# The QKV weight is transposed and centred on TensorE instead of on VectorE, ScalarE and GpSimd

## The chip, the core and the metric

The kernel runs on one core of a Trainium2 chip. Its time is the device time of one execution in microseconds (us); the times given are medians of the runs named. A profile is one execution recorded by the hardware: each row of it is an instruction, or a group of instructions of one source line (L1385 is line 1385 of the kernel before) on one engine. PE is TensorE, and PEld its weight loads; DVE is VectorE, ACT is ScalarE, POOL is GpSimd, SP issues transfers.

## The reference, cut to what matters

One transformer layer on x of 8 batches x 256 tokens x 256 columns: attention with 16 query heads, 4 key and 4 value heads of 128 columns, then a feed-forward part with 8 routed experts and a shared one. Only the start of the attention is touched:

```python
x = layernorm(x)
qkv = einsum("bsh,oh->bso", x, w_qkv)          # w_qkv: 3072 x 256
q, k, v = split(qkv, [2048, 2560], axis=-1)    # heads of 128 columns
q = (q - mean(q)) * rsqrt(var(q) + eps) * qn_g + qn_b    # over a head's 128 columns
k = (k - mean(k)) * rsqrt(var(k) + eps) * kn_g + kn_b
q = q * cos + rotate_half(q) * sin ; k likewise
```

The mean over a head's columns is linear in the weight. So the kernel takes the mean off the weight once ("centres" it), and the projected heads need no mean taken off.

## The kernel before, in words

**Tiling.** A batch has two tiles of 128 tokens. The weight comes in four groups g, one for each key head: 768 columns = key 128, four queries 512, value 128; and in two halves kk of the 256 input columns. A *unit* u is one group for one token tile: 8 units a batch, 64 in all. Each engine has its own program, an order written out by hand as a loop over steps s (two steps a unit), and waits on semaphores; no planner is at work.

**A unit.** TensorE projects it into pQ in two parts (`qkv`, lines 504 to 520: columns 0 to 511, then 512 to 767), each with six matmuls, because every f32 operand is split into a rounded "hi" part and a "lo" rest (`mm3`, lines 458 to 461). ScalarE squares each head with a running sum (`rope`, L976) and copies the value. VectorE multiplies by two rotary tables TA and TC (L1436, L1441). GpSimd (lines 2003 to 2023) takes the root of the variances (L1999, L2001), adds the two products (L2013), scales by the root (L2016) and adds a third table TB (L2023). Unit 1 alone has those last three on VectorE (`rope_end`, L1409 to L1417). TensorE then transposes the heads (`qk_T`, L527); from step 8 on the scores, the softmax and the output projection of earlier heads are woven in.

**The weight, before.** The weight arrives with the input columns on the partitions, so that it is ready to be multiplied. For each of the 8 pieces (g, kk):

- the means of its five query and key heads: on VectorE for g = 0 (`wq_mean0`, L1369, L1372), on ScalarE for the others (`wq_mean`, L939: five activations with a running sum);
- VectorE subtracts them in place (`wq_centre`, L1380);
- ScalarE rounds to the hi part (`wq_hi`, L945);
- VectorE subtracts the hi part to get the lo part (`wq_lo`, L1385); for the first piece GpSimd does this (L2170).

The steps at which the pieces of g = 2 and 3 are handled stand in the dictionaries MEAN, CENTRE, HI and LO. A unit's projection waits for the lo parts of its group (`s_wqlo_p`, `s_wqlo_d`).

**The rotary tables, before.** TA, TB and TC have five heads each for both token tiles t. GpSimd (t = 0, and TB of t = 1) and VectorE (TA and TC of t = 1, L1392) write the key's head and one query head (`put`), and ScalarE spreads the query head to the three others (`spread`, L955): six spreads.

**PSUM.** Eight banks: pQ two, pT, pS0, pS1, pP, pA, pO one each. The scores' and probabilities' banks are not used until step 8.

Of the kernel before, what the change touches and what calls it, by code (L numbers as in the profile page):

```python
# [14 lines left out]
H = 16  # L15
HKV = 4
# [99 lines left out]
def program(nc, x_d, wqkv_d, wo_d, gb_d, sw_d, ew_d, cs_d, const_d, route_d, spare_d, out_d):  # L116
    with ExitStack() as ctx:
# [31 lines left out]
        tables = part(ropes, 0, 3840).rearrange("p (v t h d) -> p v t h d", v=3, t=2, h=5)  # L149
        t2 = part(ropes, 3840, 2 * QKW).rearrange("p (z c) -> p z c", z=2)  # L150
        t1 = part(ropes, 5120, 3 * QKW).rearrange("p (z c) -> p z c", z=3)
        TA, TB, TC = (tables[:, i, :, :, :] for i in range(3))
        TAB = {"A": TA, "B": TB, "C": TC}
        const = sb("const", [128, 384])
        ident = const[:, 0:128]
        mask = const[:, 128:384]
# [7 lines left out]
        wmean = sb("wmean", [128, 4, 10])  # L164
# [46 lines left out]
        for c, (a, b) in enumerate(CHUNKS):  # L211
# [60 lines left out]
                for (a, b), p in zip(CHUNKS, (pQ[:, 768:1024], pS[1], pS[1]))]  # L272
# [16 lines left out]
        s_dconst, s_dtab = sem("s_dconst"), sem("s_dtab")  # L289
# [18 lines left out]
        s_wmean_a, s_wqhi, s_spread, s_wohi, s_swhi, s_ewhi = (  # L308
            sem(n) for n in ("s_wmean_a", "s_wqhi", "s_spread", "s_wohi", "s_swhi", "s_ewhi"))
# [26 lines left out]
        s_half, s_gain, s_tab_p, s_tabB_p, s_wqlo_p = (  # L336
            sem(n) for n in ("s_half", "s_gain", "s_tab_p", "s_tabB_p", "s_wqlo_p"))
# [118 lines left out]
        def _(e):  # L456
# [42 lines left out]
            def qkv(u, y):  # L499
# [1826 lines left out]
```

## Time and profile before

| | |
|---|---|
| time, three runs | 679.14, 680.0, 681.01 us (median 680.0) |
| span of the profiled execution, first to last instruction | 677.7 us |
| what lies around the span, by those three runs | 1.4 to 3.3 us |
| busy share of the span: PE, PEld, DVE, ACT, POOL | 93%, 86%, 83%, 83%, 82% |
| mean granted TensorE clock, share of full speed | 0.986 |
| instructions | 15538 |

The time of the profiled execution itself is not recorded apart from its span. Shares over the whole span are averages: the start, the attention (up to about 500 us) and the feed-forward part have different limits. The first 15 us are mostly transfers and the first weights.

### The profile page before, as it was taken

How to read it: one execution, taken by the hardware profiler on the slowest of the kernel's cores; microseconds unless marked ns; L12 is line 12 of the kernel's file. 1: busy time of each engine (PE TensorE's matmuls, PEld its weight loads, DVE VectorE, ACT ScalarE, POOL GpSimd, SP SyncE). 2: the span in 40 equal slices, each digit the busy share in tenths (PEclk: the TensorE clock that was granted, in tenths of full speed). 3: DMA queues.
4: the chain of work that ended last, by engine and by line, in shares of the span. 5: the costliest groups of instructions: out<-in, count | busy, mean ns of one | idle time of the engine just before them, and what ended most of it. 6: DMA issues, size and time to landing. Idle time of an engine off the chain costs nothing.

```text
span 677.7 us, 15538 instructions
## 1 busy us (share of the span) xinstructions
PE 631.1 (93%) x4430; PEld 582.2 (86%) x4430; DVE 564.6 (83%) x1925; ACT 565.3 (83%) x2175; POOL 554.9 (82%) x590
## 2 busy tenths in 40 slices
PE   3668999999999999999999999999889999999993
PEld 2557899999999999999999999899779889999981
DVE  6899999998988889888988989988989865555576
ACT  5779999999989999998999999899898536666643
POOL 5799889999999999999999998999877424666654
PEclk9789999999999999999999999999899999999998
DMA  9001023999440000000000000000346123443163
GB/s 346 7 1 33 21 83 108 334 335 291 4 46 1 2 2 2 1 1 1 2 2 1 2 1 1 2 1 25 111 132 220 56 83 116 127 127 120 71 257 124
DMA packets 50978, 54.20 MB, mean 80 GB/s; under 512 B 19824, under 2 KB 42608, under 8 KB 50768
## 3 DMA queue, kind: packets, MB, share of 16 engines
q1 hardware_dynamic: 47488, 43.84, 22.3%
q0 software_dynamic: 3408, 9.38, 3.7%
q8 instruction: 38, 0.62, 0.4%
q14 instruction: 44, 0.36, 0.2%
HBM read 23.76 MB, written 29.51 MB: 79 GB/s over the span
## 4 chain that ended last, share of the span: by engine, by line
POOL 55%; PE 26%; ACT 8%; DVE 5%; issue 4%; DMA 0%; ACTq 0%; DVEq 0%; POOLq 0%
POOL ropes L2023 12%; POOL ropes L2013 12%; POOL ropes L2016 10%; POOL rs L2001 9%; POOL hrow L2037 3%; PE pQ L459 2%; PE pQ L461 2%; PE pQ L460 2%; POOL osb L2044 2%; PE pO L459 2%; ACT ropes L976 2%; POOL rs L1999 2%; PE pO L460 2%; PE pO L461 2%; ACT P L991 2%
## 5 line engine op out<-in xcount | busy, mean ns | idle before, releaser
L459 PE MATMUL pQ<-W 128*128 128x512 f32 (+2 forms) x334 | 119.2, 357 | 10.2 <-DVE W L1385 5.3
L991 ACT ACTIVATE P<-P,nmx 128x128 f32<-128x128 f32 (+1 forms) x256 | 120.3, 502 | 0.0
L460 PE MATMUL pQ<-W 128*128 128x512 f32 (+2 forms) x334 | 114.2, 342 | 0.0
L461 PE MATMUL pQ<-W 128*128 128x512 f32 (+2 forms) x334 | 113.8, 341 | 0.0
L999 ACT ACTIVATE P<-P,rinv 128x128 f32<-128x128 f32 (+1 forms) x256 | 107.2, 492 | 2.5 <-DVE rinv L1468 2.3
L2013 POOL TENSOR_TENSOR ropes<-ropes 128x640 f32<-128x640 f32 x63 | 99.3, 1577 | 6.2 <-DVE ropes L1441 6.2
L2023 POOL TENSOR_TENSOR ropes<-ropes 128x640 f32<-128x640 f32 x63 | 100.3, 1591 | 4.9
L976 ACT ACTIVATE ropes<-pQ 128x128 f32<-128x128 f32 x320 | 89.8, 311 | 13.8 <-POOL ropes L2023 8.0
L459 PE MATMUL pO<-W 128*128 128x256 f32 (+1 forms) x323 | 95.1, 295 | 6.4 <-DVE W L1477 4.7
L1472 DVE TENSOR_TENSOR W<-pP,W 128x384 fp32r<-128x384 f32 x128 | 70.2, 549 | 29.5 <-ACT W L1004 29.2
L460 PE MATMUL pO<-W 128*128 128x256 f32 (+1 forms) x323 | 91.4, 283 | 0.0
L461 PE MATMUL pO<-W 128*128 128x256 f32 (+1 forms) x323 | 91.3, 283 | 0.0
L2016 POOL TENSOR_TENSOR ropes<-ropes,rs 128x640 f32<-128x640 f32 x63 | 81.2, 1290 | 4.9
L2001 POOL TENSOR_TENSOR rs<-rs,half 128x5 f32<-128x5 f32 x64 | 77.4, 1209 | 5.3
L459 PEld LDWEIGHTS pQ<-W 128*128 128x128 f32 x334 | 65.4, 196 | 16.5 <-issue 4.6
L976 ACT ACTIVATION_READ_ACCUMULATOR ropes<-pQ 128x1 f32 x320 | 75.7, 243 | 0.0
L459 PEld LDWEIGHTS pO<-W 128*128 128x128 f32 x323 | 61.4, 190 | 13.8 <-DVE W L1477 7.8
L461 PEld LDWEIGHTS pQ<-W 128*128 128x128 f32 x334 | 65.0, 195 | 6.0
L1004 ACT ACTIVATE W<-pP 128x384 fp32r<-128x384 f32 x128 | 67.5, 527 | 2.0 <-PE pP L551 1.7
L460 PEld LDWEIGHTS pQ<-W 128*128 128x128 f32 x334 | 65.4, 196 | 2.9
L2135 POOL DMA_INDIRECT ys<-ropes x39 | 38.9, 997 | 33.4 <-ACT ropes L1127 25.0
L551 PE MATMUL pP<-const,P 128*128 128x128 f32 x384 | 63.5, 275 | 1.3 <-DVE W L1472 1.2
(268 smaller groups left out, 2209.9 us busy)
## 6 DMA issues: line engine op xcount, KB each, us to landing
xs<-stage SPq DMA_DIRECT2D x1, 17550.0 KB, 58.4
stage<-xs SPq DMA_DIRECT2D x39, 130.0 KB, 2.3
ropes<-in_ew SPq DMA_DIRECT2D x8, 608.0 KB, 4.9
stage<-in_wqkv SPq DMA_DIRECT2D x3, 768.0 KB, 8.2
stage<-ys SPq DMA_DIRECT2D x4, 512.0 KB, 6.3
ropes<-ys SPq DMA_DIRECT2D x4, 512.0 KB, 7.5
out<-X SPq DMA_DIRECT2D x7, 256.0 KB, 2.0
X<-in_wo SPq DMA_DIRECT2D x1, 1536.0 KB, 12.8
```

What stands on the lines that cost most here:

```text
L459: e.matmul(out, lh, rh, start=start, stop=False, skip_group_check=True)
L460: e.matmul(out, lh, rl, start=False, stop=False, skip_group_check=True)
L461: return e.matmul(out, ll, rh, start=False, stop=stop, skip_group_check=True)
L976: a = e.activation(t2[:, z, h * D:h * D + D], pQ[:, h * D:h * D + D], ACT.Square, accum_out=ss[:, z, h:h + 1])
L991: a = e.activation(P[:, z, span(t)], P[:, z, span(t)], ACT.Exp, bias=nmx[:, z, t:t + 1], scale=-1.0, accum_out=sums[:, z, t:t + 1])
L999: a = e.activation(P[:, z, span(t)], P[:, z, span(t)], ACT.Copy, scale=rinv[:, z, t:t + 1])
L1004: e.activation(PT[:, 0, n % 2, :], pP[:, 0:384], ACT.Copy).then_inc(s_PThi, 1)
L1472: e.tensor_tensor(PT[:, 1, n % 2, :], pP[:, 0:384], f(PT[:, 0, n % 2, :]), ALU.subtract).then_inc(s_PT, 1)
L2001: e.tensor_tensor(dst, dst, half[:, 0:n], ALU.pow).then_inc(s_root, 1)
L2013: e.tensor_tensor(t1[:, z3, :], t1[:, z3, :], t2[:, z, :], ALU.add).then_inc(s_add, 1)
L2016: e.tensor_tensor(v3, v3, rs[:, z, :].unsqueeze(2).to_broadcast([128, 5, D]), ALU.mult).then_inc(s_mul, 1)
L2023: e.tensor_tensor(v3, v3, TB[:, t, :, :], ALU.add).then_inc(s_rope, 1)
```

## The change

TensorE now does what three engines did. The host hands the weight over with the output columns of a head on the partitions, and a second constant matrix I - 1/128 ("centring"). Multiplying a raw 128 x 128 block by it on TensorE in true f32 transposes it and takes the mean off in one product; the value's block is only transposed. `centre(i)`, i = 2g + kk, makes one piece: five f32 matmuls and one transpose into two PSUM banks that are idle at the start (those of the scores for kk = 0, those of the probabilities and the output projection for kk = 1). ScalarE's `wq_hi` and VectorE's `wq_lo` read the result from PSUM. All lo parts are VectorE's. Means, in-place centring and their two dictionaries go.

The columns of a group are now four queries, key, value. TA and TC hold one query and one key head and are read by VectorE with a broadcast over the heads; only TB is still spread (two spreads). TB of t = 1 moves from GpSimd to VectorE (`bias_table1`). The mask has its own transfer later in SP's queue, the constants come ahead of the weight, and the gains' scaling is ScalarE's first work.

```diff
-MEAN = {(2, 0): 4, (2, 1): 5, (3, 0): 7, (3, 1): 8}
-CENTRE = {(2, 0): 5, (2, 1): 5, (3, 0): 9, (3, 1): 9}
-HI = {(2, 0): 6, (2, 1): 6, (3, 0): 9, (3, 1): 10}
-LO = {(2, 0): 6, (2, 1): 7, (3, 0): 10, (3, 1): 11}
+CENTRE = {0: [2], 1: [3], 3: [4, 5], 5: [6], 6: [7]}
+HI = {1: [2], 2: [3], 4: [4], 5: [5], 6: [6], 7: [7]}
+LO = {2: [2], 3: [3], 4: [4], 5: [5], 6: [6], 7: [7]}
...
+        pSS = pb("pSS", 1024)
+        pPO = pb("pPO", 1024)
+        pW = [pSS[:, 0:GW], pPO[:, 0:GW]]
...
         @block.sync
             e.dma_start(X[:, 0:2, :], x_d[:, 0:2, :]).then_inc(s_dx[0], 16)
-            for kk in range(2):
-                e.dma_start(raw_q[0][:, kk, :], wqkv_d[:, 0, kk, :]).then_inc(s_dwq[kk], 16)
-            e.dma_start(const[:, :], const_d).then_inc(s_dconst, 16)
-            e.dma_start(cs[:, :, :, :], cs_d).then_inc(s_dtab, 16)
-            e.dma_start(gb[:, :, :], gb_d).then_inc(s_dtab, 16)
+            e.dma_start(const[:, 0:256], const_d[:, 0:256]).then_inc(s_dconst, 16)
+            e.dma_start(raw_q[0][:, 0, :], wqkv_d[:, 0, 0, :]).then_inc(s_dwq[0], 16)
+            e.dma_start(gb[:, :, :], gb_d).then_inc(s_dgb, 16)
+            e.dma_start(raw_q[0][:, 1, :], wqkv_d[:, 0, 1, :]).then_inc(s_dwq[1], 16)
+            e.dma_start(cs[:, :, :, :], cs_d).then_inc(s_dcs, 16)
             for g in range(1, HKV):
                 e.dma_start(raw_q[g], wqkv_d[:, g, :, :]).then_inc(s_dwq[g + 1], 16)
+            e.dma_start(mask, const_d[:, 256:512]).then_inc(s_dmask, 16)
...
         @block.tensor
+            def centre(i):
+                g, kk = divmod(i, 2)
+                e.wait_ge(s_dwq[kk if g == 0 else g + 1], 16)
+                if i == 0:
+                    e.wait_ge(s_dconst, 16)
+                if i >= 2:
+                    e.wait_ge(s_wqlo, i - 1)
+                for h in range(5):
+                    e.matmul(pW[kk][:, h * D:h * D + D], raw_q[g][:, kk, h * D:h * D + D], centring, start=True,
+                             stop=True, skip_group_check=True)
+                e.transpose(pW[kk][:, QKW:GW], raw_q[g][:, kk, QKW:GW], ident).then_inc(s_wcen, 1)
...
+            centre(0)
             ln1_T(0)
+            centre(1)
             for s in range(WOVEN):
                 if s < QFIRST:
                     qkv(s // 2, s % 2)
                 if 0 <= tu < NU:
                     qk_T(tu, tr)
+                for i in CENTRE.get(s, []):
+                    centre(i)
...
         @block.scalar
-            wq_hi(0, 0)
+            e.wait_ge(s_dgb, 16)
+            e.activation(gb[:, 0:2, :], gb[:, 0:2, :], ACT.Copy, scale=float(D) ** -0.5).then_inc(s_gain, 1)
+            wq_hi(0)
             ln1_hi(0)
-            e.wait_ge(s_dtab, 32)
-            e.activation(gb[:, 2:4, :], gb[:, 2:4, :], ACT.Copy, scale=float(D) ** -0.5).then_inc(s_gain, 1)
-            wq_hi(0, 1)
-            wq_mean(1, 0)
-            spread(0, "A")
-            spread(0, "C")
+            wq_hi(1)
...
+                for i in HI.get(s, []):
+                    wq_hi(i)
+                if s in (2, 3):
+                    spread(s - 2)
...
         @block.vector
+            def wq_lo(i):
+                g, kk = divmod(i, 2)
+                e.wait_ge(s_wqhi, i + 1)
+                e.tensor_tensor(WQ[:, g, 1, kk, :], pW[kk], f(WQ[:, g, 0, kk, :]), ALU.subtract).then_inc(s_wqlo, 1)
...
-                e.tensor_tensor(t1[:, z3, h0 * D:h1 * D], pQ[:, h0 * D:h1 * D],
-                                TA[:, t, h0:h1, :].rearrange("p h d -> p (h d)"), ALU.mult)
+                e.tensor_tensor(t1[:, z3, h0 * D:h1 * D].rearrange("p (h d) -> p h d", d=D),
+                                pQ[:, h0 * D:h1 * D].rearrange("p (h d) -> p h d", d=D),
+                                TA[:, t, y:y + 1, :].to_broadcast([128, n, D]), ALU.mult)
...
             ln1_stats(0)
-            wq_mean0(0)
-            wq_centre(0, 0)
             ln1_apply(0)
-            wq_mean0(1)
-            wq_centre(0, 1)
+            wq_lo(0)
             ln1_lo(0)
-            wq_lo(0, 1)
-            table1("A")
-            table1("C")
+            wq_lo(1)
+            scale_tables1()
...
                 if s == 2:
-                    wq_centre(1, 0)
-                    wq_centre(1, 1)
+                    bias_table1()
                 if s == 4:
-                    wq_lo(1, 0)
-                    wq_lo(1, 1)
                     rope_end(1)
+                for i in LO.get(s, []):
+                    wq_lo(i)
```

On GpSimd the lo part of the first piece (L2170) and TB of t = 1 go; the tables of t = 0 stay.

## Rows read from the trace of the kernel before

**Rows 1.** Whole core by stretch: busy us of each engine and (x instructions), then PE clock.
```profile
15.20:40.80 25.60, 16.71 (x71) 13.25 (x71) 22.79 (x44) 19.76 (x108) 21.02 (x21) 0.87 0.08 34
40.80:58.50 17.70, 11.94 (x66) 9.17 (x65) 17.16 (x47) 14.29 (x57) 17.22 (x14) 0.90 0.03 6
58.50:79.80 21.30, 19.97 (x138) 17.67 (x138) 21.20 (x65) 21.08 (x83) 19.09 (x16) 1.00 0.06 23
79.80:139.50 59.70, 58.91 (x435) 55.46 (x433) 54.88 (x200) 56.08 (x239) 54.70 (x52) 1.00 0.56 177
```

**Rows 2.** Timeline of POOL at the start: start us, duration us, instruction (units 0, 2, 3, 5).
```profile
20.03 1.54 POOL L2013 TENSOR_TENSOR ropes<-ropes 128x640 f32<-128x640 f32 x1
...
32.57 1.56 POOL L2013 TENSOR_TENSOR ropes<-ropes 128x640 f32<-128x640 f32 x1
...
40.87 1.55 POOL L2013 TENSOR_TENSOR ropes<-ropes 128x640 f32<-128x640 f32 x1
...
52.93 3.69 POOL L2037 TENSOR_SCALAR hrow<-X,mv,lr 128x256 f32<-128x256 f32 x2
...
58.47 1.58 POOL L2013 TENSOR_TENSOR ropes<-ropes 128x640 f32<-128x640 f32 x1
```

**Rows 3.** Waits from 15.2 to 39.2 us: in total, times, longest.
```profile
PE pQ L459 <- DVE W L1385: 4.4, 2, 3.5
...
POOL rs L1999 <- ACT ropes L976: 3.6, 1, 3.6
...
DVE ropes L1436 <- ACT ropes L976: 3.2, 3, 1.7
```

**Rows 4.** Groups by line, DVE, 15.2 to 39.2 us: busy us, mean ns, idle before.
```profile
L1385 DVE TENSOR_TENSOR W<-stage,W 128x768 fp32r<-128x768 f32 x4 | 5.4, 1364 | 0.0
...
L1380 DVE TENSOR_TENSOR stage<-stage,wmean 128x640 f32<-128x640 f32 x4 | 3.5, 912 | 0.0
```

**Rows 5.** Groups by line, DVE, 40.8 to 58.5 us.
```profile
L1385 DVE TENSOR_TENSOR W<-stage,W 128x768 fp32r<-128x768 f32 x2 | 3.2, 1593 | 0.0
L1380 DVE TENSOR_TENSOR stage<-stage,wmean 128x640 f32<-128x640 f32 x2 | 3.0, 1522 | 0.0
```

**Rows 6.** Timeline of the first 20 us, four instructions, with [idle before].
```profile
4.94 0.82 DVE L1369 TENSOR_REDUCE wmean<-stage 128x5 f32<-128x640 f32 x1
...
9.66 3.88 POOL L2029 TENSOR_TENSOR ropes<-P,osb 128x256 f32<-128x256 f32 x4
...
15.27 0.69 DVE L1436 TENSOR_TENSOR ropes<-pQ,ropes 128x512 f32<-128x512 f32 x1 [1.12 <-ACT ropes L976]
...
17.68 0.66 POOL L1999 TENSOR_SCALAR rs<-ss 128x5 f32<-128x5 f32 x1
```

**Rows 7.** Timeline of PE: matmuls at the two clocks, and one f32 product.
```profile
14.07 0.41 PE L460 MATMUL pQ<-W 128*128 128x256 f32 x1
...
14.29 0.41 PE L461 MATMUL pQ<-W 128*128 128x256 f32 x1
...
27.28 0.28 PE L460 MATMUL pQ<-W 128*128 128x256 f32 x1
...
27.40 0.28 PE L461 MATMUL pQ<-W 128*128 128x256 f32 x1
...
659.17 1.02 PE L754 MATMUL pS<-ropes,const 128*128 128x512 f32 x2
```

**Rows 8.** Timeline of POOL later on, two units in a row and one layer norm.
```profile
112.37 2.44 POOL L2037 TENSOR_SCALAR hrow<-X,mv,lr 128x256 f32<-128x256 f32 x2
...
139.46 1.57 POOL L2013 TENSOR_TENSOR ropes<-ropes 128x640 f32<-128x640 f32 x1
...
145.43 1.58 POOL L2013 TENSOR_TENSOR ropes<-ropes 128x640 f32<-128x640 f32 x1
```

**Rows 9.** Groups by line up to 54 us: ACT's means, DVE's tables.
```profile
L939 ACT ACTIVATE W<-stage 128x128 fp32r<-128x128 f32 x30 | 8.9, 315 | 0.0
...
L1392 DVE TENSOR_TENSOR ropes<-P,osb 128x128 f32<-128x128 f32 (+1 forms) x3 | 1.9, 681 | 0.0
```

More of the change, by code:

```diff
@@ L148, in program @@
         ropes = sb("ropes", [128, 7040])
-        tables = part(ropes, 0, 3840).rearrange("p (v t h d) -> p v t h d", v=3, t=2, h=5)
+        TB = part(ropes, 0, 1280).rearrange("p (t h d) -> p t h d", t=2, h=5)
+        TA = part(ropes, 1280, 512).rearrange("p (t h d) -> p t h d", t=2, h=2)
+        TC = part(ropes, 1792, 512).rearrange("p (t h d) -> p t h d", t=2, h=2)
         t2 = part(ropes, 3840, 2 * QKW).rearrange("p (z c) -> p z c", z=2)
         t1 = part(ropes, 5120, 3 * QKW).rearrange("p (z c) -> p z c", z=3)
-        TA, TB, TC = (tables[:, i, :, :, :] for i in range(3))
-        TAB = {"A": TA, "B": TB, "C": TC}
-        const = sb("const", [128, 384])
+        const = sb("const", [128, 512])
         ident = const[:, 0:128]
-        mask = const[:, 128:384]
+        centring = const[:, 128:256]
+        mask = const[:, 256:512]
         hrow = sb("hrow", [128, 2, HID])
@@ L176, in program @@
         pT = pb("pT", 512)
-        pS = [pb("pS0", 512), pb("pS1", 512)]
-        pP = pb("pP", 512)
+        pSS = pb("pSS", 1024)
+        pS = [pSS[:, 512 * z:512 * z + 512] for z in range(2)]
+        pPO = pb("pPO", 1024)
+        pP, pO = pPO[:, 0:512], pPO[:, 512:1024]
         pA = pb("pA", 512)
-        pO = pb("pO", 512)
+        pW = [pSS[:, 0:GW], pPO[:, 0:GW]]
         raw_q = [stage[:, 1536 * g:1536 * g + 1536].rearrange("p (k c) -> p k c", k=2) for g in range(HKV)]
@@ L1394, in put, with scale_tables1, bias_table1 @@
                 return a
-            def table1(which):
-                dst = TAB[which][:, 1, :, :]
-                if which == "A":
-                    e.wait_ge(s_gain, 1)
-                    put(dst, cs[:, 0, 1, :], 0, False).then_inc(s_tab_d, 1)
-                else:
-                    put(dst, cs[:, 1, 1, :], 0, True).then_inc(s_tab_d, 1)
+            def scale_tables1():
+                e.wait_ge(s_gain, 1)
+                e.wait_ge(s_dcs, 16)
+                put(TA[:, 1, :, :], cs[:, 0, 1, :], 0, False).then_inc(s_tab_d, 1)
+                put(TC[:, 1, :, :], cs[:, 1, 1, :], 0, True).then_inc(s_tab_d, 1)
+            def bias_table1():
+                put(TB[:, 1, 3:5, :], cs[:, 0, 1, :], 1, False)
+                put(ctmp[:, 1, :, :], cs[:, 1, 1, :], 1, True).then_inc(s_tab_d, 1)
+                e.wait_ge(s_tab_d, 3)
+                e.tensor_tensor(TB[:, 1, 3:5, :], TB[:, 1, 3:5, :], ctmp[:, 1, :, :], ALU.add).then_inc(s_tab_d, 1)
             def rope_end(u):
@@ L2265 @@
     i = np.arange(128)
+    centring = ident - f32(1.0 / D)
     mask = np.where(i[None, :] > i[:, None], f32(-2e38), f32(0)).astype(f32)
@@ L2315 @@
         "x": x, "wqkv": wqkv, "wo": wo, "gb": gb, "sw": sw, "ew": ew, "cs": cs,
-        "const": np.concatenate([ident, 0 * mask, mask], axis=1), "route": route,
+        "const": np.concatenate([ident, centring, 0 * mask, mask], axis=1), "route": route,
         "spare": spare,
```

141 lines of the change are left out of this document (46 added, 95 removed).

## The prediction

> **What bounds the kernel now.** I first read the busy time by stretch [rows 1]. From 79.8 us TensorE is busy 58.91 of 59.70 us: the attention proper is TensorE's, and its instructions are the same after the change. What the change touches lies earlier. From 58.5 to 79.8 VectorE has no gap (21.20 of 21.30 us), and before 58.5 no engine is the limit alone: TensorE is idle 25.60 - 16.71 = 8.9 us of the stretch from 15.2 to 40.8, and 5.8 us of the next.
>
> The waits of that first stretch [rows 3] tell why: TensorE waits 4.4 us for lo parts of the weight (L1385), GpSimd 3.6 us and VectorE 3.2 us for ScalarE's squares, which stand behind ScalarE's 30 mean activations of 0.315 us each [rows 9]. So the making of the weight sits on VectorE and ScalarE in front of the first units, while TensorE idles.
>
> How far a delay there reaches, I read from GpSimd's timeline, the chain of waits running along it: unit 0's add starts at 20.03, unit 2's at 32.57, unit 3's at 40.87, unit 5's at 58.47 [rows 2]. Later a unit alone takes GpSimd 145.43 - 139.46 = 5.97 us [rows 8]. The two units from 40.87 to 58.47 take 17.60 with one layer norm between them. GpSimd was busy for all but 0.5 us of it [rows 1], but with stretched instructions: that layer norm took 3.69 us there [rows 2] and 2.44 later [rows 8]. They stretch while VectorE subtracts with both inputs in SBUF, and VectorE's do too: the centrings of that stretch took 1.522 us each, against 0.912 in the earlier one, and the lo parts 1.593 and 1.364 [rows 4, 5].
>
> **The change, part by part.**
>
> *A f32 product on TensorE.* The trace has one kind: 512 columns by the identity, two records in 1.02 us [rows 7]. For 128 columns I take two records at the spacing of 256-column matmuls, because each record of an f32 product streams at half pace: 0.12 us at the high clock, 0.22 at the low one [rows 7]; the second spacing is that of the 1.2 GHz level, though the column of the granted clock says 1.00 there. A product then costs 0.24 us, and a piece (five products, one transpose) 1.3; at the low level 0.44 and 2.3 to 2.4. Eight pieces are some 10.5 us at the high clock.
>
> The footnote to the table of engine peaks in the Trainium skill (Perfetto Trace Analysis, Engine Utilization) gives TensorE half its output rate for an f32 product in low and high halves. The row shows two such records for each product, a quarter of the rate. By the page a piece would cost about 0.7 us, and unit 0 would come up to 1.2 us earlier than I put it; I go by the row.
>
> *Unit 0.* The first weights are in by 4.94 us at the latest, when VectorE sums them [rows 6]; the constants now go ahead of them, so I start `centre(0)` at 5.6. TensorE was idle then, so 2.3 us at the low clock cost nothing but order: the transpose of the input waits until 7.9, `centre(1)` runs from 8.9 to 11.2. ScalarE's hi (0.85) and VectorE's lo follow each. The lo part reads one operand from PSUM; the nearest row is the 512-column product of that sort, 0.69 us [rows 6], so for 768 columns at most 1.04: I take 1.0. The second lo part is then ready at about 13.1, and the first half of unit 0's projection ends between 13.9 (high clock) and 14.9 (low), so VectorE's first rotary product starts between 15.1 and 16.2, against 15.27 [rows 6]. Nothing is won up to here. `centre(2)` is queued ahead of the projection's second half and delays its squares to 16.7 (high) or 19.2 (low). GpSimd's work on unit 0 began at 17.68, after tables that began at 9.66 [rows 6]. It loses a lo part and three of the six table pieces, and ends its tables at about 14. Unit 0's add starts at 18.1 or 20.7, against 20.03.
>
> *VectorE up to unit 3.* From 15.27 to unit 3's products (39.3 us) it loses four centrings, 3.5 us; its four lo parts of 5.4 us become six of 1.0, and TB of t = 1 comes to it: four operations of about 0.68 [rows 4, 9], 2.7 us. Net 3.5 + 5.4 - 6.0 - 2.7 = 0.2 us less. What is to win is the 3.2 us of waiting for squares [rows 3]. All of it, if TensorE and ScalarE are always ahead; nothing, if VectorE now waits for TensorE's centrings instead. TensorE's six remaining pieces (2 to 7) take 7.8 us of its 8.9 idle ones at the high clock, so they fit; ScalarE loses 30 x 0.315 us and more [rows 9], so squares stand behind hi parts alone. I take half, 1.6. With 0.2 that is 1.8, and I round to 2.0 for the faster start of GpSimd. Bounds: 3.6 won (all waits gone, high clock) and 0.7 lost (no wait gone, first product 0.9 late).
>
> *Units 3 to 5.* VectorE loses 3.2 + 3.0 = 6.2 us here [rows 5]: the last two centrings are gone, and the last two lo parts are already made. With it goes what they did to GpSimd, which then paces this stretch: two units of 5.97 and a layer norm of 2.44 are 14.4 us, 3.2 less than 17.60. If the subtractions for the output weight, which stay, still stretch the layer norm to 3.69, it is 2.0 less. I take 2.6. VectorE's 17.16 - 6.2 and TensorE's 11.94 us of work [rows 1] fit in 15.
>
> *What costs nothing.* The rotary products read TA and TC by broadcast, in all units. The centring read a broadcast too, and its 640 columns took 0.912 us with contention, no more than the products' 0.69 for 512 would make; I put it at zero, covered by VectorE's 4.8 us of idle time in 79.8 to 139.5 [rows 1]. Without that cover, 0.02 us on each of 128 products would be 2.6 us. Four spreads on ScalarE go, off the path. The mask's own transfer lands long before step 8. `row_ends` and the route's transfer on SP now wait for the pieces, which are ready earlier.
>
> *The sum.* 2.0 + 2.6 = 4.6 us. From 58.5 on VectorE and then TensorE work without gaps on the same instructions, so the lead is neither eaten nor enlarged. The profiled span of 677.7 becomes 673.1; the median of the three runs lies 2.3 above that span, and so I forecast 675.4. The bounds, -0.7 + 2.0 = 1.3 and 3.6 + 3.2 = 6.8 us, are 678.7 and 673.2.
>
> A measurement of this kernel can tell about 0.3%, 2.0 us, from no change.
>
> **The rivals.**
>
> *The lead is given back* (679 to 681). If, past 58.5, the pace is not the work but a wait that stays where it is, all is hidden. For it: VectorE's 21.20 of 21.30 us looks like a floor, and the subtractions for the output weight fall into that stretch, in a new overlap with GpSimd. Against it: that work is not tied to a clock time; it begins when the steps before it end. Its transfer was issued at the start and is long there.
>
> *TensorE becomes the bound of the start* (slower). If the clock stays at the low level while it centres, the six pieces take 13.8 to 14.4 us, and 8.9 of idle time don't hold them: some 4.9 us or more stand in front of unit 3 instead of the 2.0 won. With half of the 2.6 behind it still won, that is 3.6 us slower, 683.6. It decides from a piece of 8.9 / 6 = 1.5 us on, little above my 1.3. For it: TensorE ran long parts of this start at the low level [rows 7], and the mean clock of 0.87 shows it [rows 1]. Against it: the centrings fill the very gaps after which the clock had fallen, and at the high clock TensorE's own matmuls of this stretch shrink too.
>
> *More than forecast* (under 673). If GpSimd isn't the pace from unit 3 to 5, VectorE's whole 6.2 us count, up to 3.6 + 6.2 = 9.8 us, 670.2. ScalarE's 14.29 us in that stretch [rows 1], only some 1.7 of them hi parts that move away, speak against most of it.
>
> *The broadcast costs.* If VectorE reads a repeated operand slower, every unit pays, but TensorE is the pace there: it would need more than the 4.8 us of slack to show. I put it with the slower cases, at 682.6 if its 2.6 us came on top.
>
> **How the numbers follow.** The forecast's case, 1.3 to 6.8 us won: 0.70, of which 0.06 goes to the part under 2.0 us. More than 6.8: 0.07. Given back, within 2 us of 680.0: 0.13. TensorE the bound: 0.06; the broadcast and what I don't see: 0.04. So faster 0.64 + 0.07 = 0.71, same 0.06 + 0.13 = 0.19, slower 0.10. The range, 672.5 to 680.0, leaves out the larger gain, the slower cases and the upper edge of the hidden case; the forecast's own is 673.2 to 678.7.
>
> **What the profile after would show.** Right: pieces of 1.3 us on TensorE in its former gaps; the wait of TensorE for L1385 shorter than 4.4 us; unit 3's add on GpSimd near 38.9 us and unit 5's near 53.9; from there the same distances as before, with VectorE's products no longer than 0.69 us. Wrong in the first term, if unit 3's add is not earlier than 40.87; in the second, if units 3 to 5 still take 17 us; in the carrying, if unit 5's add is 4 us earlier and the end is not. The forecast fails as a whole if a piece takes 2 us on TensorE throughout, or if another engine, ScalarE first, has no gap from 40 us on.

## The result, and the profile after

The changed kernel takes 674.81 us (median of four runs, 673.5 to 675.87; before 679.9 in the same session). The ratio is 0.9925, interval 0.9909 to 0.9941: 4.0 to 6.2 us faster. The forecast was 675.4. The profiled execution took 675.87 us with a span of 673.8, 3.9 less than the 677.7 before.

The busy time by stretch answers to [rows 1]; the columns are the same.

```profile
15.20:40.80 25.60, 20.43 (x141) 17.65 (x139) 22.17 (x49) 15.13 (x67) 18.63 (x18) 1.00 0.12 51
40.80:58.50 17.70, 14.32 (x82) 12.00 (x80) 15.63 (x52) 15.81 (x64) 17.06 (x15) 0.90 0.09 31
58.50:79.80 21.30, 20.39 (x145) 18.28 (x145) 21.30 (x67) 20.67 (x84) 18.26 (x14) 1.00 0.06 14
79.80:139.50 59.70, 59.17 (x432) 55.62 (x432) 54.88 (x204) 56.02 (x235) 54.72 (x53) 1.00 0.63 199
```

From 15.2 to 40.8 TensorE is busy 20.43 us instead of 16.71, at a granted clock of 1.00 instead of 0.87, and ScalarE 15.13 instead of 19.76. VectorE is hardly freer (22.17 for 22.79) in that stretch; it does more of the attention in it.

GpSimd's timeline answers to [rows 2]: unit 0, the next products of units 2 and 3, the layer norm, units 5, 8 and 63.

```profile
18.25 1.81 POOL L1990 TENSOR_TENSOR ropes<-ropes 128x640 f32<-128x640 f32 x1
...
30.79 1.56 POOL L1990 TENSOR_TENSOR ropes<-ropes 128x640 f32<-128x640 f32 x1 [1.44 <-DVE ropes L1427]
32.44 1.26 POOL L1993 TENSOR_TENSOR ropes<-ropes,rs 128x640 f32<-128x640 f32 x1
...
35.40 0.19 POOL L1976 TENSOR_SCALAR lr<-mv 128x2 f32<-128x2 f32 x1
...
37.89 1.57 POOL L1990 TENSOR_TENSOR ropes<-ropes 128x640 f32<-128x640 f32 x1
...
48.36 2.89 POOL L2014 TENSOR_SCALAR hrow<-X,mv,lr 128x256 f32<-128x256 f32 x2
...
53.03 1.57 POOL L1990 TENSOR_TENSOR ropes<-ropes 128x640 f32<-128x640 f32 x1
...
60.05 1.57 POOL L1990 TENSOR_TENSOR ropes<-ropes 128x640 f32<-128x640 f32 x1 [0.61 <-DVE ropes L1427]
...
75.23 1.57 POOL L1990 TENSOR_TENSOR ropes<-ropes 128x640 f32<-128x640 f32 x1 [0.89 <-DVE ropes L1427]
...
475.54 1.58 POOL L1990 TENSOR_TENSOR ropes<-ropes 128x640 f32<-128x640 f32 x1
```

The same view of the kernel before, for what [rows 2] don't show:

```profile
34.21 1.85 POOL L2016 TENSOR_TENSOR ropes<-ropes,rs 128x640 f32<-128x640 f32 x1
...
37.79 0.78 POOL L1999 TENSOR_SCALAR lr<-mv 128x2 f32<-128x2 f32 x1
...
79.82 1.57 POOL L2013 TENSOR_TENSOR ropes<-ropes 128x640 f32<-128x640 f32 x1 [0.90 <-DVE ropes L1441]
...
480.14 1.58 POOL L2013 TENSOR_TENSOR ropes<-ropes 128x640 f32<-128x640 f32 x1
```

The reading that carries the rest is to take differences between units. Unit 0's add comes 1.78 us earlier. From there to unit 2 both kernels take 12.54, which is a coincidence, as VectorE's timeline below shows. From unit 2 to unit 3 it is 7.10 instead of 8.30, and the 1.20 are two instructions: the product with the root takes 1.26 instead of 1.85, the first step of a root 0.19 instead of 0.78. From unit 3 to 5 it is 15.14 instead of 17.60. That makes a lead of 5.44 at unit 5. Between units 5 and 8 GpSimd waits for VectorE's product, and 0.85 is given back; from unit 8 (4.59) to unit 63 (4.60) nothing changes. In the traces of the twelve kernels below the lead grows by 0.37 to 0.55 between these two, so half a microsecond is within what single traces leave open.

The waits from 15.2 to 39.2 us answer to [rows 3].

```profile
ACT ropes L986 <- PE pQ L461: 7.7, 4, 3.2
POOL rs L1976 <- ACT ropes L986: 5.7, 2, 3.0
...
PE pPO L472 <- DVE W L1364: 1.7, 2, 1.2
...
PE pSS L472 <- DVE W L1364: 1.4, 2, 1.3
...
DVE ropes L1421 <- ACT ropes L986: 1.4, 2, 1.0
```

TensorE's 4.4 us for lo parts have become 3.1, now in front of the pieces (L472) instead of the projections. VectorE waits 1.4 for squares instead of 3.2, but GpSimd 5.7 instead of 3.6: unit 2's squares are late because ScalarE waits 7.7 us for TensorE in this stretch. Why, TensorE's timeline tells (pieces 0, 2 and 5, and unit 2's projection):

```profile
6.28 2.50 PE L472 MATMUL pSS<-const,stage 128*128 128x128 f32 x10 [6.28 <-DMA stage<-in_wqkv]
...
14.05 1.28 PE L472 MATMUL pSS<-const,stage 128*128 128x128 f32 x10
15.17 0.27 PE L474 MATMUL pSS<-const,stage 128*128 128x128 f32 x1
15.19 0.36 PE L459 MATMUL pQ<-W 128*128 128x256 f32 x1
...
22.28 1.35 PE L472 MATMUL pPO<-const,stage 128*128 128x128 f32 x10 [1.17 <-DVE W L1364]
...
23.49 0.47 PE L459 MATMUL pQ<-W 128*128 128x512 f32 x1
```

Each f32 product is two records. A piece at the high clock holds TensorE 15.19 - 14.05 = 1.14 us, while piece 0, at the 1.2 GHz level, takes twice that (the level is read from the spacing of its records; the clock column says 1.00 there). Unit 2's projection stands behind piece 5, and piece 5 behind a lo part.

These late squares don't set unit 2, though. With its root done, GpSimd waits another 1.44 us for VectorE's product (30.79 above). VectorE's timeline in the changed kernel (its first product, and its last for unit 2), its busy time between, and its last product for unit 2 in the kernel before:

```profile
15.43 0.69 DVE L1421 TENSOR_TENSOR ropes<-pQ,ropes 128x512 f32<-128x512 f32 x1 [0.95 <-ACT ropes L986]
...
30.43 0.28 DVE L1427 TENSOR_TENSOR ropes<-pQ,ropes 128x128 f32<-128x128 f32 x1
```

```profile
19.98:30.79 10.81, 7.74 (x57) 6.62 (x56) 10.66 (x18) 5.36 (x20) 6.11 (x7) 1.00 0.01 2
```

```profile
32.01 0.28 DVE L1441 TENSOR_TENSOR ropes<-pQ,ropes 128x128 f32<-128x128 f32 x1
```

VectorE is busy for 10.66 of the 10.81 us up to unit 2's add: it sets unit 2 now. From its first product (15.43, before 15.27) to this last one it takes 15.00 us instead of 16.74. So unit 2's 1.78 us come from VectorE's shorter waits, not from the earlier unit 0, behind which GpSimd waits again.

### The profile page after: what moved, and what is told of

It is laid out like the page before. It is cut to its first block, busy times and chain, and to the rows that moved or that the text cites. A ratio compares the mean times of both kernels' runs of the same rounds, so it can differ in the third digit from the quotient of the medians.

```text
span 673.8 us, 15649 instructions
## 1 busy us (share of the span) xinstructions
PE 636.3 (94%) x4518; PEld 589.2 (87%) x4518; DVE 553.9 (82%) x1918; ACT 555.4 (82%) x2111; POOL 543.9 (81%) x585
## 4 chain that ended last, share of the span: by engine, by line
POOL 50%; PE 28%; ACT 9%; DVE 6%; issue 5%; DMA 1%; SPq 0%; ACTq 0%; DVEq 0%; POOLq 0%
POOL ropes L1990 11%; POOL ropes L2000 11%; POOL ropes L1993 9%; POOL rs L1978 9%; PE pQ L459 3%; POOL hrow L2014 3%; PE pQ L461 3%; PE pQ L460 3%; ACT ropes L986 2%; POOL osb L2021 2%; PE pPO L459 2%; ACT P L1001 2%; PE pPO L460 2%; PE pPO L461 2%; POOL rs L1976 1%
## 5 line engine op out<-in xcount | busy, mean ns | idle before, releaser
L459 PE MATMUL pQ<-W 128*128 128x512 f32 (+2 forms) x334 | 116.4, 349 | 2.1 <-DVE W L1364 0.8
L460 PE MATMUL pQ<-W 128*128 128x512 f32 (+2 forms) x334 | 111.8, 335 | 0.0
L461 PE MATMUL pQ<-W 128*128 128x512 f32 (+2 forms) x334 | 111.4, 333 | 0.0
L459 PE MATMUL pPO<-W 128*128 128x256 f32 (+1 forms) x323 | 95.7, 296 | 5.6 <-DVE W L1465 3.6
L1460 DVE TENSOR_TENSOR W<-pPO,W 128x384 fp32r<-128x384 f32 x128 | 70.2, 549 | 30.2 <-ACT W L1014 30.0
L460 PE MATMUL pPO<-W 128*128 128x256 f32 (+1 forms) x323 | 91.9, 285 | 0.0
L461 PE MATMUL pPO<-W 128*128 128x256 f32 (+1 forms) x323 | 91.7, 284 | 0.0
L459 PEld LDWEIGHTS pPO<-W 128*128 128x128 f32 x323 | 61.9, 192 | 12.8 <-DVE W L1465 6.7
L459 PEld LDWEIGHTS pQ<-W 128*128 128x128 f32 x334 | 63.6, 190 | 6.6 <-DVE W L1364 1.2
L1014 ACT ACTIVATE W<-pPO 128x384 fp32r<-128x384 f32 x128 | 67.1, 524 | 2.4 <-PE pPO L565 2.2
L461 PEld LDWEIGHTS pQ<-W 128*128 128x128 f32 x334 | 63.3, 190 | 5.6
L460 PEld LDWEIGHTS pQ<-W 128*128 128x128 f32 x334 | 63.7, 191 | 2.6
L1437 DVE TENSOR_TENSOR W<-pT,W 128x384 fp32r<-128x384 f32 (+1 forms) x128 | 61.5, 480 | 5.2 <-ACT W L994 5.1
```

Source lines behind the costliest of these rows:

```text
L459: e.matmul(out, lh, rh, start=start, stop=False, skip_group_check=True)
L460: e.matmul(out, lh, rl, start=False, stop=False, skip_group_check=True)
L461: return e.matmul(out, ll, rh, start=False, stop=stop, skip_group_check=True)
L1014: e.activation(PT[:, 0, n % 2, :], pP[:, 0:384], ACT.Copy).then_inc(s_PThi, 1)
L1460: e.tensor_tensor(PT[:, 1, n % 2, :], pP[:, 0:384], f(PT[:, 0, n % 2, :]), ALU.subtract).then_inc(s_PT, 1)
```

## The experiments

Every kernel below was timed against the kernel before, in sessions of one to four kernels; the kernel before took 679.86 to 680.61 us in them (medians). The changed kernel was timed only in its own session, so it is compared with the others by the ratios; where two intervals overlap, the times don't tell the two kernels apart. The table gives the differences in GpSimd's timeline (us), the lead over the kernel before at units 8 and 63, and the times. In the changed kernel and its variants the first weights land between 5.9 and 6.9 us, so a single trace places unit 0 to about half a microsecond; the differences between units don't hang on that.

| kernel | unit 0 | 0 to 2 | 2 to 3 | 3 to 5 | 5 to 8 | lead at 8 | at 63 | time | ratio, interval |
|---|---|---|---|---|---|---|---|---|---|
| before | 20.03 | 12.54 | 8.30 | 17.60 | 21.35 | | | 679.9 | |
| after | 18.25 | 12.54 | 7.10 | 15.14 | 22.20 | 4.59 | 4.60 | 674.81 | 0.9925, 0.9909 to 0.9941 |
| tables_alone | 17.96 | 17.48 | 8.27 | 17.60 | 21.35 | -2.84 | -2.32 | 682.01 | 1.0025, 1.0012 to 1.0039 |
| weight_alone | 18.02 | 12.60 | 7.09 | 15.12 | 21.34 | 5.65 | 6.03 | 674.46 | 0.9922, 0.9907 to 0.9936 |
| warm_before | 20.89 | 13.26 | 8.29 | 17.58 | 21.36 | -1.56 | -1.07 | 681.85 | 1.0031, 1.0017 to 1.0044 |
| double_centre | 23.06 | 14.27 | 7.81 | 15.11 | 21.36 | -1.79 | -1.24 | 679.3 | 0.9995, 0.9985 to 1.0005 |
| act_mean | 19.04 | 12.91 | 7.67 | 15.11 | 22.20 | 2.89 | 3.41 | 675.24 | 0.9926, 0.9911 to 0.994 |
| dve_sub | 18.85 | 12.54 | 7.08 | 17.64 | 21.36 | 2.35 | 2.72 | 675.86 | 0.9937, 0.9921 to 0.9953 |
| dve_red | 18.32 | 12.55 | 7.08 | 14.84 | 22.22 | 4.81 | 5.21 | 674.43 | 0.991, 0.9896 to 0.9924 |
| transp | 16.27 | 12.66 | 7.11 | 15.12 | 21.46 | 7.20 | 7.73 | 673.35 | 0.9906, 0.9885 to 0.9927 |
| tb_pool | 17.70 | 12.62 | 7.08 | 15.13 | 22.21 | 5.08 | 5.47 | 674.07 | 0.9912, 0.9896 to 0.9929 |
| warm_start | 17.30 | 12.55 | 7.08 | 15.12 | 21.37 | 6.40 | 6.84 | 672.56 | 0.9895, 0.9877 to 0.9913 |
| all_four | 17.06 | 12.15 | 7.08 | 15.14 | 21.35 | 7.04 | 7.52 | 673.32 | 0.9918, 0.9898 to 0.9939 |
| order4 | 18.63 | 13.55 | 7.11 | 15.13 | 22.21 | 3.19 | 3.61 | 675.61 | 0.9941, 0.9927 to 0.9954 |

**The two halves apart.** *tables_alone* is the kernel before with only the new order of columns, the narrow tables, the broadcast reads and TB of t = 1 on VectorE:

```diff
-            spread(0, "A")
-            spread(0, "C")
...
-                e.tensor_tensor(t1[:, z3, h0 * D:h1 * D], pQ[:, h0 * D:h1 * D],
-                                TA[:, t, h0:h1, :].rearrange("p h d -> p (h d)"), ALU.mult)
+                e.tensor_tensor(t1[:, z3, h0 * D:h1 * D].rearrange("p (h d) -> p h d", d=D),
+                                pQ[:, h0 * D:h1 * D].rearrange("p (h d) -> p h d", d=D),
+                                TA[:, t, y:y + 1, :].to_broadcast([128, n, D]), ALU.mult)
...
+                    bias_table1()
```

*weight_alone* is the changed kernel with the old five-head tables and six spreads, and TB of t = 1 on GpSimd:

```diff
-                if s == 2:
-                    bias_table1()
...
+                if s == 2:
+                    spread(1, "A")
+                    spread(1, "C")
```

> The kernel before with only the table half of the change: query columns first, TA and TC with two heads read by broadcast, two spreads instead of six, TB of t = 1 on VectorE; the weight is prepared as before. Theory W (the lead comes from the weight's preparation leaving VectorE and ScalarE): ScalarE loses four spreads of about 0.55 us, VectorE gets about 1.4 us more, so the time stays within 1 us of the kernel before, about 679.5. Rival T (the lead comes from the smaller tables, which free GpSimd and the squares early): 3 to 5 us faster, 675 to 677.

> The changed kernel with the five-head tables, the six spreads and GpSimd's table work of before put back; the weight is still transposed and centred on TensorE. Theory W: 4 to 5 us faster than before, 675 to 676; unit 3's add on GpSimd still near 38 to 39 us. Rival T: no more than 1 us faster than before, 679 to 680.

The weight half alone gives all of the gain; the table half alone makes the kernel slower, by 2 us where theory W had less than 1. The waits of tables_alone from 15.2 to 39.2 us say where:

```profile
POOL rs L2000 <- ACT ropes L974: 9.7, 3, 7.7
...
PE pQ L459 <- DVE W L1379: 6.0, 1, 6.0
```

VectorE makes TB while the lo parts for unit 2 wait behind it, and the work around it stretches (the two centrings ahead of it take 2.91 us instead of 1.94, the two lo parts 3.07 instead of 1.82). So TensorE's wait for these lo parts grows from 4.4 to 6.0 us and units 0 to 2 take 17.48 us. Either half alone brings unit 0 two microseconds forward, since each takes work from GpSimd's queue ahead of it (a lo part, or TB).

**Is it the clock?** *warm_before* is the kernel before with as many f32 products of the identity, unused, put into TensorE's gaps at the places of the pieces.

```diff
+            def idle_work(i):
+                out = [pS[0], pP][i % 2]
+                for h in range(5):
+                    e.matmul(out[:, 128 * (h % 4):128 * (h % 4) + 128], ident, ident, start=True, stop=True,
...
+                for i in {0: [2], 1: [3], 3: [4, 5], 5: [6], 6: [7]}.get(s, []):
+                    idle_work(i)
```

> The kernel before, with TensorE doing 8 x 5 f32 products of the identity into the idle banks at the places where the changed kernel centres; nobody reads them, and VectorE, ScalarE and GpSimd work as before. Rival C (the lead comes from TensorE's clock, which rises some 8 us earlier because TensorE has work in its gaps): 2 to 4 us faster than before, 676 to 678. Theory W: the matmuls of units 0 to 3 get shorter but wait for the same lo parts, so within 1 us of before, 679 to 681.

```profile
15.20:40.80 25.60, 19.75 (x114) 16.78 (x114) 23.45 (x39) 18.51 (x100) 21.14 (x20) 0.87 0.08 32
```

Slower by 2 us, with units 2 to 3 and 3 to 5 as before: work in TensorE's gaps alone gains nothing. It doesn't settle the clock, for the granted clock of this stretch stayed at 0.87, as before the change, and was 1.00 in the changed kernel. What the higher clock is worth by itself, no run isolates.

**What a piece costs.** *double_centre* issues each of the five products twice (the second overwrites the first).

```diff
-                for h in range(5):
+                for h in [0, 1, 2, 3, 4] * 2:
                     e.matmul(pW[kk][:, h * D:h * D + D], raw_q[g][:, kk, h * D:h * D + D], centring, start=True,
```

> The changed kernel with every f32 product of the centring done twice, so that a piece takes some 2.5 us instead of 1.3 at the high clock. TensorE is idle 5.2 us of 15.2 to 40.8 in the changed kernel, and six pieces bring 7.2 more there. Theory (the piece's price decides from about 1.5 us on, as the prediction has it): 2 to 4 us slower than the changed kernel, 677 to 679. Rival (the pieces hide in TensorE's waits whatever they take): under 1 us slower, up to 675.8.

*transp* has five plain transposes instead of the products, so the centring is left out and the heads keep their means.

```diff
-                    e.matmul(pW[kk][:, h * D:h * D + D], raw_q[g][:, kk, h * D:h * D + D], centring, start=True,
+                    e.transpose(pW[kk][:, h * D:h * D + D], raw_q[g][:, kk, h * D:h * D + D], ident)
```

> The changed kernel with five plain transposes in place of the five f32 products of a piece: the centring is left out, so the heads' means are not taken off. A piece should take about 0.7 us at the high clock and 1.3 at the low one instead of 1.3 and 2.5. Theory H (TensorE's centring is hidden in its gaps but for the first two pieces): unit 0's add about 1 to 1.5 us earlier than 18.25, unit 3's add 0.5 to 1.5 us earlier than 37.9, the kernel 673.3 to 674.5. Rival B (the six later pieces still hold TensorE and with it units 1 to 3): unit 3's add 3 us or more earlier, the kernel under 672.5. Rival N (nothing of the centring is on the path): within 0.5 us of 674.8.

Timeline of TensorE in transp, pieces 0 and 2:

```profile
5.94 1.33 PE L472 MATMUL pSS<-const,stage 128*128 128x128 f32 x5 [5.94 <-DMA stage<-in_wqkv]
...
12.28 0.71 PE L472 MATMUL pSS<-const,stage 128*128 128x128 f32 x5
```

A piece takes half, and what is won is in unit 0 (16.27); up to unit 5 the distances stay as they were. So at the high clock the five later pieces cost nothing, and the first three, which stand in front of unit 0's two projections, do (the medians don't tell this kernel from the changed one). Doubled pieces cost 4.81 us in unit 0 and 2.44 between units 0 and 3 in the trace, which took longest of its twelve executions, and 4.5 us in the medians, more than expected. TensorE is then busy 23.78 of the 25.60 us:

```profile
15.20:40.80 25.60, 23.78 (x181) 21.78 (x180) 18.14 (x37) 11.48 (x48) 12.01 (x12) 1.00 0.12 48
```

**Whose work was the brake?** Three kernels put one thing each back into the changed kernel, unused: ScalarE's thirty means (*act_mean*), four subtractions on VectorE with both operands in SBUF at the steps of the last centrings and lo parts (*dve_sub*), and sums over the same columns there, with one operand (*dve_red*).

The edit of act_mean, and that of dve_sub:

```diff
+            wq_mean(1, 0)
...
+                for g, kk in {2: [(1, 1)], 4: [(2, 0)], 5: [(2, 1)], 7: [(3, 0)], 8: [(3, 1)]}.get(s, []):
+                    wq_mean(g, kk)
```

```diff
+                for kk, n in {9: [(0, 640), (1, 640)], 10: [(0, 768)], 11: [(1, 768)]}.get(s, []):
+                    e.tensor_tensor(raw_q[3][:, kk, 0:n], raw_q[3][:, kk, 0:n], raw_q[2][:, kk, 0:n], ALU.subtract)
```

In dve_red the last line is a sum instead:

```diff
+                    e.tensor_reduce(wsum[:, 2 * (n > 640) + kk, 0:n // D], raw_q[3][:, kk, 0:n].rearrange("p (h d) -> p h d", d=D), AXX,
+                                    ALU.add)
```

> The changed kernel, with ScalarE's thirty mean activations (about 0.32 us each, 9.4 us in all) put back at the steps they had before; nobody reads their results. Theory S (the first term was ScalarE's time: squares stood behind the means): the squares come late again, unit 3's add on GpSimd goes from 37.9 back to 40.5 to 41 us, VectorE waits about 3 us for squares between 15.2 and 39.2, and the kernel takes 677.3 to 678.3 us, the first term of the lead lost and the second kept. Rival V (the first term was VectorE's own centrings and lo parts): unit 3's add within 0.5 us of 37.9, time within 0.7 us of 674.8.

> The changed kernel, with four subtractions of two SBUF operands (two of 640, two of 768 columns) put back on VectorE at the steps where the last two centrings and lo parts stood; results unused. Theory G (between units 3 and 5 these four set the pace, by their time and by stretching GpSimd): unit 3's add stays at 37.9, units 3 to 5 take 17 to 17.6 us again instead of 15.1, the layer norm on GpSimd takes 3.7 us again or more, and the kernel takes 677 to 677.8 us, the second term lost. Rival O (units 3 to 5 got faster by something else, the moved hi parts on ScalarE or the clock): units 3 to 5 within 0.5 us of 15.1, time within 0.7 us of 674.8.

> As the kernel with the four subtractions put back, but each is a sum over the same columns with one SBUF input and a small output, so about the same time on VectorE (0.7 to 0.8 us each, 3.1 us in all) without a second operand. Theory C (the stretch of GpSimd by two-operand work is what cost): units 3 to 5 take at most 15.6 us and the kernel 674.8 to 675.8. Theory P (VectorE's own time paces units 3 to 5 whatever it does): units 3 to 5 take about 18 us less what is idle, some 16.5 to 18, and the kernel 676.5 to 678.

First the two on VectorE. GpSimd's timeline (unit 3, layer norm, unit 5) and VectorE's groups from 36 to 60 us in dve_sub:

```profile
38.47 1.57 POOL L1994 TENSOR_TENSOR ropes<-ropes 128x640 f32<-128x640 f32 x1
...
50.57 3.68 POOL L2018 TENSOR_SCALAR hrow<-X,mv,lr 128x256 f32<-128x256 f32 x2
...
56.11 1.58 POOL L1994 TENSOR_TENSOR ropes<-ropes 128x640 f32<-128x640 f32 x1
```

```profile
L1829 DVE TENSOR_TENSOR stage<-stage 128x768 f32<-128x768 f32 x2 | 2.9, 1458 | 0.0
...
L1829 DVE TENSOR_TENSOR stage<-stage 128x640 f32<-128x640 f32 x2 | 1.9, 1013 | 0.0
```

and the same in dve_red:

```profile
37.95 1.57 POOL L1996 TENSOR_TENSOR ropes<-ropes 128x640 f32<-128x640 f32 x1
...
48.92 2.46 POOL L2020 TENSOR_SCALAR hrow<-X,mv,lr 128x256 f32<-128x256 f32 x2
...
52.79 1.57 POOL L1996 TENSOR_TENSOR ropes<-ropes 128x640 f32<-128x640 f32 x1
```

```profile
L1830 DVE TENSOR_REDUCE wsum<-stage 128x6 f32<-128x768 f32 x2 | 1.9, 952 | 0.0
...
L1830 DVE TENSOR_REDUCE wsum<-stage 128x5 f32<-128x640 f32 x2 | 1.5, 815 | 0.0
```

Four subtractions of 4.8 us bring units 3 to 5 back to 17.64, the layer norm back to 3.68. Sums of 3.4 us over the same columns at the same steps leave 14.84 and 2.46. So in the traces the brake is the second SBUF operand, by what it does to GpSimd, and not VectorE's time. By the Trainium skill (SBUF — State Buffer, Who interferes with whom) a VectorE instruction with two SBUF inputs contends with a GpSimd instruction that reads SBUF, because its second input comes through a read interface that the two share, and one with at most one SBUF input, outside the two-port modes, does not. The two rows of the layer norm agree: 3.68 against 2.46 us. The subtractions also write wide results and the sums don't, but the changed kernel's lo parts write 768 columns from one SBUF operand, and GpSimd's root beside one of them (from 21.64 us) takes 1.18 us, against 1.63 and 1.76 beside two-operand work in the kernel before. In the medians dve_sub lies 1.4 us above dve_red (the executions hardly overlap) and 1.1 above the changed kernel: less than the 2.5 of the traces, and short of theory G's 677 to 677.8. The profiled execution of dve_sub took longest of its six, so how much of the second term the other executions gained stays open.

act_mean's waits from 15.2 to 39.2 us:

```profile
POOL rs L1991 <- ACT ropes L998: 10.5, 3, 5.4
...
DVE ropes L1436 <- ACT ropes L998: 2.4, 2, 1.5
```

Unit 3's add is 1.73 us later (39.62), of which 0.79 stand at unit 0, where piece 1 ran longer at the low level (2.26 us instead of 1.60): less than the 2.6 to 3.1 of the theory, more than its rival's 0.5. Its median (675.24) can't be told from the changed kernel's, although its trace is 1.2 us behind at unit 63; there too the profiled execution took longest. What the means cost the untraced executions stays open.

**Can more be had?** *tb_pool* makes TB of t = 1 on GpSimd again, with the narrow tables. *warm_start* puts fourteen products of a blank block on TensorE while the first transfers run. *order4* moves piece 5 behind unit 2's first projection. *all_four* has all three, and ScalarE rounds piece 0 before it scales the gains.

The three edits in this order:

```diff
-                if s == 2:
-                    bias_table1()
...
-            put(TB[:, 0, 3:5, :], cs[:, 0, 0, :], 1, False)
+            for t in range(2):
+                put(TB[:, t, 3:5, :], cs[:, 0, t, :], 1, False)
```

```diff
+            e.wait_ge(s_blank, 1)
+            for i in range(14):
+                e.matmul(pT[:, 0:128], blank, blank, start=True, stop=True, skip_group_check=True)
             centre(0)
```

```diff
-CENTRE = {0: [2], 1: [3], 3: [4, 5], 5: [6], 6: [7]}
+CENTRE = {0: [2], 1: [3], 3: [4], 4: [5], 5: [6], 6: [7]}
```

> The changed kernel with its narrow tables and broadcast reads, but the third table TB of the second token tile is made on GpSimd again, as before the change. Theory B (the table half's cost is VectorE's four operations for TB in front of unit 1): unit 8's add on GpSimd comes 0.8 to 1.3 us earlier than 75.23, as with the old tables (74.17), and the kernel takes 673.5 to 674.5 us. Rival R (the cost is in the broadcast reads or the fewer spreads, not in where TB is made): unit 8's add within 0.3 us of 75.23 and the time within 0.5 us of 674.8.

> The changed kernel, with fourteen f32 products of a blank 128 x 128 block put on TensorE ahead of the first piece, while the first transfers are under way; nothing reads them. Theory K (the first two pieces took 2.5 and 1.6 us because TensorE came from idleness at the lower clock level, and unit 0 waits for them): the ten records of the first piece take about 1.3 us instead of 2.50, unit 0's add comes 0.8 to 1.3 us earlier than 18.25, and the kernel takes 673.5 to 674.3 us. Rival L (the lower level is not a matter of what ran before, or unit 0 waits for the transfers): the first piece again 2.5 us, or unit 0's add within 0.3 us of 18.25; time within 0.5 us of 674.8.

> The two edits above together (TB of the second tile on GpSimd, fourteen blank products ahead of the first piece), and two more: piece 5 is put on TensorE one step later, behind unit 2's projection, and ScalarE rounds piece 0 before it scales the gains. If the gains add up, unit 0's add is at about 17.0, unit 8's at 72.5 to 73.3 instead of 75.23, and the kernel takes 672.0 to 673.3 us. Rival: VectorE, without a gap from 58.5 on in the changed kernel, already sets units 5 to 8, and what comes earlier in front of it is waited away: unit 8's add at 74 or later, time 673.8 or more.

> The changed kernel with one piece moved: piece 5 is put on TensorE one step later, behind unit 2's first projection instead of ahead of it. In the trace of the changed kernel unit 2's projection starts at 23.49 us, 1.4 us after its last lo part was done (22.13), because piece 5 stands in front of it. Theory Q (TensorE's queue holds unit 2 there): from unit 0's add to unit 2's the time falls from 12.54 us to 11.1 to 12.1, unit 2's projection starts at 22.2 to 22.5, and the lead reaches unit 8; time 673.4 to 674.4 us. Rival V (VectorE sets unit 2: its last steps for unit 1, the 640-column product of 2.08 us among them, stand in front of unit 2's products): 12.3 to 12.6 us, time within 0.5 us of 674.8.

warm_start is the fastest, 679.91 - 672.56 = 7.35 us below the kernel before in its session; its interval of the ratio just touches the changed kernel's. TensorE's first two pieces in it:

```profile
6.87 1.38 PE L474 MATMUL pSS<-const,stage 128*128 128x128 f32 x10 [0.57 <-DMA stage<-in_wqkv]
...
8.90 1.38 PE L474 MATMUL pPO<-const,stage 128*128 128x128 f32 x10
```

Piece 0 takes 1.38 instead of 2.50 us, and although its weights landed 0.59 us later than in the trace of the changed kernel, unit 0's add comes 0.95 earlier. The 0.85 given back between units 5 and 8 is gone too. tb_pool gains 0.49 at unit 8, less than expected, all of it in unit 0, where a single trace can't tell; its median can't be told from the changed kernel's. all_four leads by another 0.64 at unit 8 but is not faster than warm_start in the medians.

order4 failed in an instructive way. Unit 2's projection starts at 21.69 instead of 23.49, as Q wanted, yet units 0 to 2 take 13.55 us. TensorE's timeline (piece 6) and the stretch:

```profile
27.79 2.40 PE L472 MATMUL pSS<-const,stage 128*128 128x128 f32 x10 [1.96 <-DVE W L1364]
```

```profile
15.20:40.80 25.60, 21.51 (x138) 18.86 (x136) 21.25 (x47) 14.58 (x65) 17.30 (x17) 0.93 0.11 45
```

VectorE took no notice of the earlier projection: its first product for unit 2 starts 7.21 us after its first for unit 1 (27.56 and 20.35), in the changed kernel 7.23 (27.21 and 19.98). So far rival V was right, that VectorE sets unit 2. The extra microsecond comes behind that: TensorE idled 1.96 us for VectorE's lo part, piece 6 then ran at the 1.2 GHz level, 2.40 us instead of 1.35, and VectorE waited 1.12 us for a copy of ScalarE's whose transposes stood behind piece 6. Neither theory had that. The wait alone doesn't decide it: in all_four, which has the same order after a warm start, TensorE waits the same 1.96 us, piece 6 takes 1.35, the clock stayed at 1.00 in this stretch and the distance is 12.15. order4's median, 675.61, can't be told from the changed kernel's.

## Why the prediction was right, step by step

**The piece.** Forecast 1.3 us at the high clock and 2.3 to 2.4 at the low one; measured 1.14 (15.19 - 14.05) and 2.51 (from 6.28 to the next matmul at 8.79). The row's quarter rate held. By the half rate in the Trainium skill's footnote (Perfetto Trace Analysis, Engine Utilization) a product would, as an estimate, take what a transpose takes. The trace disagrees: in transp five transposes are five records in 0.71 us, in the changed kernel five products ten records in 1.28.

**Unit 0.** The add was put at 18.1 or 20.7; it came at 18.25. VectorE's first rotary product came at 15.43 (forecast 15.1 to 16.2), the lo part from PSUM took 0.95 us (forecast 1.0). TB's four operations took VectorE 1.31 us in all (forecast 2.7).

**The first term: right in its place, mis-sized by a cause that I had left out.** I put 2.0 us up to unit 3's add; it is 2.98. Up to unit 2 the mechanism is the forecast's, and so is the size: 1.78 us, VectorE's waits for squares shrinking by 1.8 (3.2 to 1.4) while its work hardly changes. The 1.8 us of unit 0 were rightly not counted on top: GpSimd waits again behind them, 3.02 us for squares and 1.44 for VectorE, where it waited 3.60 before. That I took half of the 3.2 us was a guess that came out. How much of it is owed to the higher clock is open: the first 512 columns of unit 1's projection take TensorE 1.47 us (from 17.13) instead of 2.72 (from 16.62), and no run separates that from the work taken off ScalarE and VectorE. The other 1.20 us are GpSimd's instructions between units 2 and 3, which no longer stretch. I had seen that stretching only behind unit 3 [rows 5, 8]; it was at work ahead of it too. The kernels that keep the old centring on VectorE there take 8.27 to 8.30 us for this step, the changed kernel and most of its variants 7.08 to 7.11.

**The second term: right.** 2.6 forecast, 17.60 - 15.14 = 2.46 measured, and the traces of dve_sub and dve_red show its cause; in the medians less of it can be seen. The layer norm still takes 2.89 us, so part of the bound's 3.2 is left.

**The carrying.** "Neither eaten nor enlarged" is true from unit 8 to unit 63 (4.59, 4.60). Between units 5 and 8 it missed 0.85, which is lost in four of the variants too and not in the others. VectorE's product is late there, and the traces show behind what: the third of its subtractions for the output weight, which has both operands in SBUF and falls beside GpSimd's adds. In the changed kernel and in warm_start:

```profile
56.10 2.01 DVE L1469 TENSOR_TENSOR W<-X,W 128x512 fp32r<-128x512 f32 x1
```

```profile
54.67 0.84 DVE L1474 TENSOR_TENSOR W<-X,W 128x512 fp32r<-128x512 f32 x1
```

It takes 1.49 to 2.01 us in the five kernels with the loss and 0.83 to 0.92 in the nine without. No run isolates it, but the clock doesn't sort the kernels: from 40.8 to 58.5 it was 0.90 in the changed kernel, 0.90 in the kernel before, which has no loss, and 1.00 in dve_red, which has it. Forecast lead 4.6, measured 4.60 at unit 63: the misses, +0.98, -0.14 and -0.85, cancelled, and that the two figures agree so closely is luck.

**The end.** The profiled spans differ by 3.9 and the medians by 5.1, on either side of the lead of 4.6. In the changed kernel's trace, which took longest of its four executions, 0.6 us are lost just behind unit 63: one of GpSimd's indirect transfers starts at 489.45 us, against 493.42 before, a lead of 3.97. In the other traces the change between unit 63 and the end lies between 0.7 us won and 1.4 lost, so a lead in one trace tells the span to about a microsecond. The forecast added 2.3 us from span to median; where both are recorded, time and span lie 1.8 to 2.2 apart. The executions of the kernel before that ran at a mean granted clock of 0.987 took 678.66 to 679.53 us, those at 0.979 or less 679.31 to 682.2; its profiled one was at 0.986, and the changed kernel's runs were at 0.989 to 0.992. Part of the medians' difference may come from there; no run isolates it.

**What costs nothing.** The broadcast reads: right. VectorE's products of 512 columns from 79.8 us on, before and after:

```profile
L1436 DVE TENSOR_TENSOR ropes<-pQ,ropes 128x512 f32<-128x512 f32 x55 | 37.4, 679 | 0.0
```

```profile
L1421 DVE TENSOR_TENSOR ropes<-pQ,ropes 128x512 f32<-128x512 f32 x54 | 36.7, 680 | 0.0
```

TB on VectorE was rightly charged to VectorE, but it is only cheap because the centring has left: without that (tables_alone) the whole costs 2 us.

**The rivals.** The lead was not given back, but for 0.85, and that went the way this rival had named: the subtractions for the output weight in a new overlap with GpSimd. TensorE as the bound was the right danger: it takes doubled pieces to make it (23.78 of 25.60 us busy), or a piece at the lower clock, as order4 had. The changed kernel has 1.28 us of waiting before piece 6 and stays at the high clock.

## What to carry to other kernels

Follow one event of each unit through the stages and take differences, and ask at each what the event waited for last. Equal differences (12.54 and 12.54) don't show that nothing was won where the engine idles between the two events; here VectorE's timeline showed what had been. An engine's instruction can cost another engine more than its own time; moving two-operand SBUF work to TensorE and PSUM gained here, by the traces, mainly because GpSimd's instructions no longer stretched. And when work is put on TensorE at the start, look at the clock it will run at: blank products ahead of it were worth more here than the finer points of order.

## What the runs showed that was not expected

- The first piece at the 1.2 GHz level took 2.50 us and held unit 0; fourteen blank products ahead of it brought it to 1.38 us, and the kernel took 672.56 us instead of 674.81 (different sessions).
- An earlier projection won nothing. VectorE, which sets unit 2, kept its pace, and TensorE's next piece, after a wait of 1.96 us, ran at the lower level (2.40 us); after a warm start the same wait left it at 1.35.
- A two-operand subtraction on VectorE that stays in the kernel took 2.01 us instead of 0.84 when the change moved it beside GpSimd's adds, and went with 0.85 us of the lead.
- The lo part read from PSUM (0.95 us for 768 columns) is as fast as a one-operand sum over 768 columns in SBUF (0.952), while the two-operand subtraction beside GpSimd took 1.458.
